# Half as many broadcast rows before a graph attention, over four PSUM banks, with two transfers issued earlier

## The chip, the cores and the metric

The kernel runs on one core of a Trainium2 chip. The metric is the device time of one execution in microseconds (us). TensorE (PE) multiplies matrices, PEld is its weight load, VectorE (DVE), ScalarE (ACT) and GpSimd (POOL) do elementwise work, SyncE (SP) issues the transfers (DMA).

## What is computed

A layer norm over a first graph layer (nodes `x`, 3327 x 128, padded here to 26 tiles of 128 rows, 3328), then a second layer norm over a gated graph attention layer. Only the second layer is touched by the change. Cut to its core:

```python
hp = (adj > 0) @ hW ; hm = (adj < 0) @ hW                      # adj without its diagonal
e_plus  = leaky_relu(concat([hp, hm], 1) @ a, 0.2)[:, 0]       # one number per node and head
e_minus = leaky_relu(concat([hm, hp], 1) @ a, 0.2)[:, 0]
att = where(adj > 0, e_plus[None, :], NEG_INF)
att = where(adj < 0, e_minus[None, :], att)
att = softmax(att, axis=1)
support = sum over 3 heads of (att * adj) @ hW / 3
```

Every entry of `adj` in the given inputs is zero or between 0.05 and 1: none is negative. The kernel computes the right thing for negative entries too, in branches on a flag that is read from the data.

## The kernel before, in words

`program` (L2481) calls three stages one after the other, each a block at whose end all engines meet at a barrier: `layer0` (about 1515 us of the span), `normalize_and_sum` (L1628) and `attention_and_gates` (L2134).

`normalize_and_sum` goes over the 26 row tiles of `adjT`. For each, PE makes the node support (`g_sp`, L1755) and the sums for the scores (`g_ep`, L1777 and L1778), and ACT copies both out in `copy_sums` (L1815 to L1821), into 128 columns of `nsT` and a slice of `raw`, and raises `sums_copied`. That semaphore starts at 2, so it stands at 26 after 24 tiles and at 28 after all. SP loads the tiles (L1714, four buffers), then stores `hT` (L1719), waits for `sums_copied` to reach T + 2 = 28, stores the whole of `nsT` (L1721) and waits until both stores have landed (`stored`), before it goes to the barrier. DVE ends with `epm` (L1918): six numbers per node, three heads for positive entries and three for negative ones.

`attention_and_gates` begins with a spread: `EB` (128 x 6 x 3328) holds for each of the six a row of 3328 numbers, the same on all 128 partitions. PE makes it by transposing a column of `epm` that is broadcast to 128 x 128 against the identity (L2264), up to four transposes into one PSUM bank; such a bank is a group, 7 groups to a row (six of 4 transposes, one of 2), 42 groups. Two banks are used in turn. ACT copies the even groups to `EB` (L2338), DVE the odd ones (L2402). On DVE the copies stand behind the reading of the flag (L2393 to L2397: four register loads and an ALU chain), on PE the first transposes of attention stand behind them and behind the load of `W`. SP issues at the start of this block the first row tile of `adj` (L2217), `W`, the second tile and seven pieces of `adjT`.

Then for each of 26 row tiles and 3 heads: DVE masks the tile (once per tile, `masks`, L2407 to L2422) and makes logits and their maximum (L2436), ACT the exponential (L2347), PE transposes the 128 x 3328 result in seven pieces (L2281), DVE multiplies each with its piece of `adjT` (L2458), and PE multiplies it with `H` (L2322). DVE makes the logits two heads ahead. The first logits wait for the last copy of `EB` and for the first tile of `adj`. In `masks` and `logits` an `If` on the flag holds what negative entries need; with the given inputs it is jumped over. After 26 tiles come the gates (`gates_and_output`), which use `EB` as room.

Of the kernel before, what the change touches and what calls it, by code (L numbers as in the profile page):

```python
# [10 lines left out]
ACT = mybir.ActivationFunctionType  # L11
AX = mybir.AxisListType

P = 128
# [1610 lines left out]
                        taken_batch()  # L1625


def normalize_and_sum(nc, d, dims, H, ident, diag, epm, negs):  # L1628


    N, NP, T = dims
# [4 lines left out]
    with ExitStack() as ctx:  # L1636
# [64 lines left out]
        with nc.Block() as block:  # L1701
            @block.sync
            def _(eng):
                eng.dma_start(X[:, :, :], d["x_rows"]).then_inc(x_loaded, 16)
                eng.dma_start(shift[:, :], d["ln_b"].partition_broadcast(P)).then_inc(x_loaded, 16)
                eng.dma_start(gain[:, :], d["ln_g"].partition_broadcast(P)).then_inc(x_loaded, 16)
                eng.dma_start(WT[:, :, :], d["gat_WT"]).then_inc(loaded, 16)
                eng.dma_start(av[:, :, :], d["gat_a"]).then_inc(loaded, 16)

                def load(r, q):  # L1710
                    t = r * BUFS + q

                    eng.wait_ge(adj_free, t + 1)
                    eng.dma_start(adj[q][:, :], d["adjT"][bass.ds(t * P, P), :]).then_inc(adj_loaded[q], 16)  # L1714

                over_tiles(eng, load)

                eng.wait_ge(hT_ready, NC)
                eng.dma_start(d["hT"], hT[:, :]).then_inc(stored, 16)  # L1719
                eng.wait_ge(sums_copied, T + 2)  # L1720
                eng.dma_start(d["nsT"], nsT[:, :]).then_inc(stored, 16)  # L1721
                eng.wait_ge(stored, 32)

            @block.gpsimd
            def _(eng):
# [405 lines left out]
    return early_loads, late_load_and_stores, products, gates, blends  # L2131


def attention_and_gates(nc, d, dims, H, ident, diag, epm, negs):  # L2134

    N, NP, T = dims
    HEADS = 3
# [7 lines left out]
    with ExitStack() as ctx:  # L2145
        sb, ps, sem = scope(nc, ctx)
        EB = sb("EB", [P, 2 * HEADS, NP])
        adj = [sb(f"a_adj{i}", [P, NP]) for i in range(2)]
        adjT = sb("a_adjT", [P, NP])
        negmask = sb("negmask", [P, NP], mybir.dt.uint8)  # L2150
        prob = [sb(f"prob{i}", [P, NP]) for i in range(HEADS)]
# [16 lines left out]
        acc, rt, sup = acc_bank[:, 0:P], small_bank[:, 0:P], small_bank[:, P:2 * P]  # L2168

        loaded = sem("a_loaded")  # L2170
        adj_loaded = [sem(f"a_adj_loaded{i}") for i in range(2)]
        adjT_loaded = [sem(f"a_adjT_loaded{c}") for c in range(NC)]
        eb_turned = sem("a_eb_turned")
        eb_copied = [sem(f"a_eb_copied{i}") for i in range(2)]
# [13 lines left out]

        early_loads, late_load_and_stores, products, gates, blends = gates_and_output(
            ctx, nc, d, dims, H, ident, diag, EB, [t[:, :] for t in prob], tr + [acc_bank, small_bank], gs_stored, sup_copied)  # L2190
        EB_GROUPS = 2 * HEADS * NC

        def width(c):
            return min(512, NP - c * 512)
# [17 lines left out]
        with nc.Block() as block:  # L2212
            @block.sync
            def _(eng):
                for k in range(2):
                    eng.sem_inc(gs_stored[k], 16)
                eng.dma_start(adj[0][:, :], d["adj"][0:P, :]).then_inc(adj_loaded[0], 16)  # L2217
                eng.dma_start(W[:, :, :], d["gat_W"]).then_inc(loaded, 16)
                eng.dma_start(adj[1][:, :], d["adj"][P:2 * P, :]).then_inc(adj_loaded[1], 16)
                for c in range(NC):  # L2220
                    sl = slice(c * 512, c * 512 + width(c))
                    eng.dma_start(adjT[:, sl], d["adjT"][0:P, sl]).then_inc(adjT_loaded[c], 16)

                def store(p, k):
                    t = p * 2 + k
                    eng.wait_ge(sup_copied, t + 1)
                    eng.dma_start(d["gsT"][:, bass.ds(t * P, P)], gs[k][:, :]).then_inc(gs_stored[k], 16)

                def after(p, k, more_rows, more_turned):
                    if more_rows:  # L2230
                        eng.wait_ge(logit_ready, seq(p, k * HEADS + HEADS - 1) + 1)
                        eng.dma_start(adj[k][:, :], d["adj"][bass.ds((p * 2 + k + 2) * P, P), :])\
                           .then_inc(adj_loaded[k], 16)
                    if more_turned:
                        for c in range(NC):
                            sl = slice(c * 512, c * 512 + width(c))
                            eng.wait_ge(pT_ready, chunk(p, (k * HEADS + HEADS - 1) * NC + c) + 1)
                            eng.dma_start(adjT[:, sl], d["adjT"][bass.ds((p * 2 + k + 1) * P, P), sl])\
                               .then_inc(adjT_loaded[c], 16)

                after(0, 0, True, True)
                store(0, 0)
                after(0, 1, True, True)
                with eng.Fori(1, PAIRS - 1) as p:
                    store(p - 1, 1)
                    after(p, 0, True, True)
                    store(p, 0)
                    after(p, 1, True, True)
                store(PAIRS - 2, 1)
                after(PAIRS - 1, 0, False, True)  # L2250
                eng.wait_ge(logit_ready, seq(PAIRS, 0))
                early_loads(eng)
                store(PAIRS - 1, 0)
                store(PAIRS - 1, 1)
                late_load_and_stores(eng)

            @block.tensor
            def _(eng):
                for g in range(EB_GROUPS):
                    h, c = g // NC, g % NC  # L2260
                    if g >= 2:
                        eng.wait_ge(eb_copied[g % 2], g // 2)
                    for j in blocks(c):
                        mm = eng.transpose(tr[g % 2][:, (j % 4) * P:(j % 4 + 1) * P],  # L2264
                                           epm[:, j, h:h + 1].to_broadcast([P, P]), ident[:, :])
                    mm.then_inc(eb_turned, 1)
                for i in range(2):
                    eng.wait_ge(eb_copied[i], EB_GROUPS // 2)
                eng.wait_ge(loaded, 16)

                def turn(p, g, first, last_read):
# [62 lines left out]
            def _(eng):  # L2334
                for g in range(0, EB_GROUPS, 2):
                    h, c = g // NC, g % NC
                    eng.wait_ge(eb_turned, g + 1)
                    eng.activation(EB[:, h, c * 512:c * 512 + width(c)], tr[g % 2][:, 0:width(c)], ACT.Copy)\  # L2338
                       .then_inc(eb_copied[0], 1)

                def exp(p, n):
# [48 lines left out]
            def _(eng):  # L2390
# [8 lines left out]
                for g in range(1, EB_GROUPS, 2):  # L2399
                    h, c = g // NC, g % NC  # L2400
                    eng.wait_ge(eb_turned, g + 1)
                    eng.tensor_copy(EB[:, h, c * 512:c * 512 + width(c)], tr[g % 2][:, 0:width(c)])\  # L2402
                       .then_inc(eb_copied[1], 1)
                eng.drain()
                eng.wait_ge(eb_copied[0], EB_GROUPS // 2)

                def masks(p, k):  # L2407

# [2 lines left out]
                    block_ = adj[k][:, bass.ds((p * 2 + k) * P, P)]  # L2411
                    with eng.If(eng.snap(flag) > 0):

                        eng.tensor_tensor(dblock[:, :], block_, ident[:, :], ALU.mult)
                        eng.drain()
                        eng.tensor_tensor(block_, block_, dblock[:, :], ALU.subtract)
# [63 lines left out]
def program(nc, d, dims):  # L2480
    N, NP, T = dims  # L2481
    with ExitStack() as ctx:
# [4 lines left out]
        diag = sb("diag", [P, T])  # L2487
        epm = sb("epm", [P, T, 6])
        negs = sb("negs", [P, T])
        normalize_and_sum(nc, d, dims, H, ident, diag, epm, negs)  # L2490
        attention_and_gates(nc, d, dims, H, ident, diag, epm, negs)


# [43 lines left out]
```

## Time and profile before

| | us |
|---|---|
| median of 3 runs | 2671.07 (2668.92 to 2672.51) |
| the profiled execution | 2673.42 |
| its span in the trace | 2671.6 |
| end of `normalize_and_sum`: last copy of sums to the first instruction of attention | 1787.73 to 1793.86 |
| the spread of `epm` into `EB` | 1793.86 to 1824.75 |
| first logits to first transposes of attention | 1825.24 to 1835.16 |
| the attention proper, to the gates | to about 2569 |

Times inside the span are us from its start. Busy shares over the whole span are PE 87%, DVE 80%, ACT 40%; they are averages over stages with different limits, and the change touches two short stretches, so it is read from those stretches. The trace's "issue" is time in which an engine waited for nothing that the profile shows; a q behind an engine's name is its sequencer.

### The profile page before, as it was taken

Reading aid. Unit: us, or ns where it says so; the run is one execution under the profiler, and the core shown is the slowest. Engines: PE = TensorE matmul, PEld = TensorE weight load, DVE = VectorE, ACT = ScalarE, POOL = GpSimd, SP = SyncE. Lnnn points to the kernel's source line nnn. Section 1 sums busy time; section 2 is a strip of 40 time slices with the busy share of each in tenths; the row PEclk is TensorE's granted clock in tenths of the full one; section 3 lists DMA queues with packets and bytes.
Section 4 is the critical chain, followed back from the end, with each engine's and each line's share of the span. In section 5 each row is a group of like instructions: output and inputs, shape, how many; then the busy total and the mean of one; then the engine's idle time right before and its main releaser. Section 6 shows DMA issues by size and latency. Waiting matters only on the chain. (4 is left out here: it accounts for less than half of the span.)

```text
span 2671.6 us, 53662 instructions
## 1 busy us (share of the span) xinstructions
PE 2328.7 (87%) x17795; PEld 1971.7 (74%) x17795; DVE 2145.3 (80%) x6600; ACT 1069.8 (40%) x1803; POOL 156.8 (6%) x342
## 2 busy tenths in 40 slices
PE   7999999879889979988967369987999999999995
PEld 2666666657777867777757369976999999999962
DVE  4777777578787888888889677757999999999956
ACT  5666666443434444334431220004443333444333
POOL 0000000111111111110000100000000000000000
PEclk8999999989999989999988769999999999999997
DMA  4000000022223322222302226542343333433320
GB/s 134 2 2 1 1 1 1 2 103 78 92 91 118 116 78 104 101 80 89 119 27 103 98 96 221 205 175 84 110 142 114 130 130 104 135 125 116 119 92 26
DMA packets 57309, 244.87 MB, mean 92 GB/s; under 512 B 6929, under 2 KB 18576, under 8 KB 43344
## 3 DMA queue, kind: packets, MB, share of 16 engines
q1 hardware_dynamic: 57040, 241.99, 25.9%
q8 instruction: 83, 1.36, 0.2%
q14 instruction: 186, 1.52, 0.2%
HBM read 235.15 MB, written 6.82 MB: 91 GB/s over the span
## 5 line engine op out<-in xcount | busy, mean ns | idle before, releaser
L2322 PE MATMUL a_acc<-H,pT 128*128 128x128 f32 x4056 | 547.8, 277 | 11.6 <-ACT a_rows L2355 3.8
L2322 PEld LDWEIGHTS a_acc<-H,pT 128*128 128x128 f32 x4056 | 495.3, 192 | 28.6 <-DVE pT L2458 20.1
L994 PE MATMUL small<-XR,wT 128*128 128x128 f32 x2756 | 378.5, 283 | 27.3 <-ACT wT L1264 26.7
L994 PEld LDWEIGHTS small<-XR,wT 128*128 128x128 f32 x2756 | 344.3, 197 | 43.2 <-ACT wT L1264 43.2
L865 PE MATMUL lg<-kT,qs 128*128 128x512 f32 (+1 forms) x742 | 339.1, 593 | 27.0 <-ACT e L1182 16.8
L75 DVE MAX8 cand<-e 128x8 f32<-128x64 f32 (+3 forms) x1898 | 303.0, 241 | 50.9 <-issue 27.5
L2458 DVE TENSOR_TENSOR pT<-a_tr,a_adjT 128x512 f32<-128x512 f32 (+1 forms) x546 | 316.6, 645 | 22.2 <-PE a_tr L2281 19.1
L2281 PE MATMUL a_tr<-ident,prob 128*128 128x128 f32 x2028 | 311.4, 274 | 10.9 <-ACTq L2349 10.9
L1264 ACT ACTIVATE wT<-tr 128x512 f32<-128x512 f32 (+1 forms) x371 | 206.5, 566 | 267.3 <-PE tr L984 266.4
L894 PE MATMUL accR<-XR,adj 128*128 128x129 f32 x2704 | 313.4, 276 | 0.0
L894 PEld LDWEIGHTS accR<-XR,adj 128*128 128x128 f32 x2704 | 309.2, 193 | 0.0
L2436 DVE CUSTOM_DVE_ANT_0 prob<-a_adj,EB 128x3328 f32<-128x3328 f32 x78 | 282.6, 3623 | 0.0
L984 PE MATMUL tr<-ident,e 128*128 128x128 f32 x1378 | 216.6, 285 | 59.3 <-DVE scalars L1519 53.5
L865 PEld LDWEIGHTS lg<-kT,qs 128*128 128x128 f32 x742 | 118.4, 193 | 185.7 <-ACT e L1182 142.5
L984 PEld LDWEIGHTS tr<-ident,e 128*128 128x128 f32 x1378 | 168.3, 147 | 110.7 <-DVE scalars L1519 56.2
L1182 ACT ACTIVATE e<-lg 128x512 f32<-128x512 f32 (+1 forms) x371 | 206.6, 566 | 106.7 <-PE lg L865 104.9
L2281 PEld LDWEIGHTS a_tr<-ident,prob 128*128 128x128 f32 x2028 | 241.1, 142 | 11.1 <-issue 11.1
L2347 ACT ACTIVATE prob<-prob,a_negmax 128x3328 f32<-128x3328 f32 x78 | 239.0, 3064 | 9.1 <-DVE a_negmax L2445 9.1
L1755 PE MATMUL g_sp<-g_adj,H 128*128 128x128 f32 x1352 | 162.7, 282 | 17.1 <-ACTq L1820 17.1
L1755 PEld LDWEIGHTS g_sp<-g_adj,H 128*128 128x128 f32 x1352 | 158.5, 198 | 18.8 <-issue 18.2
L1214 ACT ACTIVATE e<-e,scalars 128x3327 f32<-128x3327 f32 x53 | 162.0, 3059 | 8.7 <-DVE scalars L1583 8.6
L224 DVE SCALAR_TENSOR_TENSOR work<-cand,mid 128x416 f32<-128x416 f32 (+1 forms) x172 | 127.3, 774 | 9.8 <-issue 3.2
(351 smaller groups left out, 2427.9 us busy)
## 6 DMA issues: line engine op xcount, KB each, us to landing
adj<-in_adjT SPq DMA_DIRECT2D x52, 1664.0 KB, 7.2
g_adj<-in_adjT SPq DMA_DIRECT2D x26, 1664.0 KB, 7.0
a_adj<-in_adj SPq DMA_DIRECT2D x26, 1664.0 KB, 6.8
a_adjT<-in_adjT SPq DMA_DIRECT2D x156, 256.0 KB, 3.9
a_adjT<-in_adjT SPq DMA_DIRECT2D x26, 128.0 KB, 4.4
XT<-in_x_t SPq DMA_DIRECT2D x1, 1664.0 KB, 7.2
hT_scratch<-hT SPq DMA_DIRECT2D x1, 1664.0 KB, 12.1
nsT_scratch<-nsT SPq DMA_DIRECT2D x1, 1664.0 KB, 5.3
```

What stands on the lines that cost most here:

```text
L75: eng.max(cand[:, n, :], src[:, n * seg:min((n + 1) * seg, width)])
L865: eng.matmul(lg[bank(st, p, k, c)][:, 0:sl.stop - sl.start], qs[k][:, :], kT[:, sl], start=True, stop=True).then_inc(lg_ready, 1)
L894: mm = eng.matmul(accR[:, :], adj[k][:, j * P:(j + 1) * P], xf[:, j, :], start=False, stop=(j == T - 1))
L984: mm = eng.transpose(tr[(k * NC + c) % 2][:, o:o + P], e[b][k][:, j * P:(j + 1) * P], ident[:, :])
L994: mm = eng.matmul(accA[:, :], wT[(k * NC + c - 1) % 2][:, o:o + P], xa[:, j, 0:P], start=(j == 0), stop=(j == T - 1))
L1182: eng.activation(e[b][k][:, sl], lg[bank(st, p, k, c)][:, 0:sl.stop - sl.start], ACT.Copy).then_inc(lg_free, 1)
L1755: mm = eng.matmul(sp[k][:, :], H[:, j, :], adj[q][:, j * P:(j + 1) * P], start=(j == 0), stop=(j == T - 1))
L2281: mm = eng.transpose(tr[g % BANKS][:, (j % 4) * P:(j % 4 + 1) * P], prob[order[n][1]][:, j * P:(j + 1) * P], ident[:, :])
L2322: mm = eng.matmul(acc[:, :], pT[g % RING][:, (j % 4) * P:(j % 4 + 1) * P], H[:, j, :], start=(j == 0), stop=(j == T - 1))
L2347: eng.activation(prob[h][:, :], prob[h][:, :], ACT.Exp, bias=negmax[h][:, :], accum_out=den[h][:, :])
L2436: eng.tensor_tensor_reduce(prob[h][:, :], adj[k][:, :], EB[:, h, :], 1.0, -3.0e38, ALU.add, ALU.max, mx[h][:, :])
L2458: eng.tensor_tensor(pT[g % RING][:, 0:width(c)], tr[g % BANKS][:, 0:width(c)], adjT[:, c * 512:c * 512 + width(c)], ALU.mult).then_inc(pT_ ...
```

## The change

1. `EB_GROUPS` is 3 x 7 = 21 in place of 42: only the three rows for positive entries are spread, over four PSUM banks (`EB_BANKS`) in place of two. ACT copies 11 groups, DVE 10; a group waits for the copy of the group four before it.
2. The rows for negative entries are made by a new function, `spread_minus`, on DVE alone, inside the flagged branch of the first tile's `masks`: three loops, jumped over where the flag is zero.
3. The first row tile of `adj` gets its own buffer, `first_adj`, and its load is issued in the stage before, behind the last load of `adjT` and ahead of the store of `hT`.
4. The store of `nsT` is split: columns 0 to 3071 once `sums_copied` is at 26, the last 256 columns (128 KB) at 28. The wait on `stored` is for all three.

```diff
@@ normalize_and_sum, SP
                 over_tiles(eng, load)
 
+                eng.dma_start(first_adj[:, :], d["adj"][0:P, :]).then_inc(first_adj_loaded, 16)
                 eng.wait_ge(hT_ready, NC)
                 eng.dma_start(d["hT"], hT[:, :]).then_inc(stored, 16)
+                most = NP - 2 * P
+                eng.wait_ge(sums_copied, T)
+                eng.dma_start(d["nsT"][:, 0:most], nsT[:, 0:most]).then_inc(stored, 16)
                 eng.wait_ge(sums_copied, T + 2)
-                eng.dma_start(d["nsT"], nsT[:, :]).then_inc(stored, 16)
-                eng.wait_ge(stored, 32)
+                eng.dma_start(d["nsT"][:, most:NP], nsT[:, most:NP]).then_inc(stored, 16)
+                eng.wait_ge(stored, 48)
@@ attention_and_gates
-        adj = [sb(f"a_adj{i}", [P, NP]) for i in range(2)]
+        adj = [first_adj, sb("a_adj1", [P, NP])]
...
-        EB_GROUPS = 2 * HEADS * NC
+        EB_GROUPS = HEADS * NC
+        EB_BANKS = 4
+        by_engine = [-(-EB_GROUPS // 2), EB_GROUPS // 2]
@@ SP
-                eng.dma_start(adj[0][:, :], d["adj"][0:P, :]).then_inc(adj_loaded[0], 16)
                 eng.dma_start(W[:, :, :], d["gat_W"]).then_inc(loaded, 16)
@@ PE
-                    if g >= 2:
-                        eng.wait_ge(eb_copied[g % 2], g // 2)
+                    if g >= EB_BANKS:
+                        eng.wait_ge(eb_copied[g % 2], (g - EB_BANKS) // 2 + 1)
                     for j in blocks(c):
-                        mm = eng.transpose(tr[g % 2][:, (j % 4) * P:(j % 4 + 1) * P],
+                        mm = eng.transpose(tr[g % EB_BANKS][:, (j % 4) * P:(j % 4 + 1) * P],
                                            epm[:, j, h:h + 1].to_broadcast([P, P]), ident[:, :])
@@ DVE
+                def spread_minus():
+
+                    quarters = [slice(q, q + 32) for q in range(0, P, 32)]
+                    for h in range(HEADS):
+                        with eng.Fori(0, T) as t:
+                            eng.tensor_copy(dblock[:, 0:32], epm[:, bass.ds(t, 1), HEADS + h].to_broadcast([P, 32]))
+                            eng.drain()
+                            eng.transpose(dblock[:, 32:64], dblock[:, 0:32])
+                            eng.drain()
+                            for n, own in enumerate(quarters):
+                                for to in quarters:
+                                    eng.tensor_copy(EB[to, HEADS + h, bass.ds(t * P + 32 * n, 32)], dblock[own, 32:64])
+                            eng.drain()
...
                     with eng.If(eng.snap(flag) > 0):
 
+                        if isinstance(p, int) and p == 0 and k == 0:
+                            spread_minus()
```

On SP, around the end of `normalize_and_sum` and the start of attention, before:

```order
L1714 DMA g_adj<-in_adjT 128x3328 [waits g_adj_free] x2
L1719 DMA hT_scratch<-hT 128x3328 [waits g_hT_ready]
L1721 DMA nsT_scratch<-nsT 128x3328 [waits g_sums_copied]
L1701 UNCONDITIONAL_BRANCH [waits g_stored]
L2213 UNCONDITIONAL_BRANCH [waits barrier_Pool_Activation_PE_DVE_SP_release]
L2217 DMA a_adj<-in_adj 128x3328
L2218 DMA gat_W_s<-in_gat_W 128x384
L2219 DMA a_adj<-in_adj 128x3328
```

and now:

```order
L1714 DMA g_adj<-in_adjT 128x3328 [waits g_adj_free] x2
L1718 DMA first_adj<-in_adj 128x3328
L1720 DMA hT_scratch<-hT 128x3328 [waits g_hT_ready]
L1723 DMA nsT_scratch<-nsT 128x3072 [waits g_sums_copied]
L1725 DMA nsT_scratch<-nsT 128x256 [waits g_sums_copied]
L1701 UNCONDITIONAL_BRANCH [waits g_stored]
L2219 UNCONDITIONAL_BRANCH [waits barrier_Pool_Activation_PE_DVE_SP_release]
L2223 DMA gat_W_s<-in_gat_W 128x384
L2224 DMA a_adj<-in_adj 128x3328
```

The first tile's load has moved ahead of the barrier and of the store of `hT`, and most of the store of `nsT` stands on a wait of its own. On DVE, at the start of attention, before:

```order
L66 TENSOR_LOAD a_flag_int x4
L67 ISA
L2402 COPY EB<-a_tr 128x512 [waits a_eb_turned] x6
L2402 COPY EB<-a_tr 128x256 [waits a_eb_turned]
L2402 COPY EB<-a_tr 128x512 [waits a_eb_turned] x6
L2402 COPY EB<-a_tr 128x256 [waits a_eb_turned]
L2402 COPY EB<-a_tr 128x512 [waits a_eb_turned] x6
L2402 COPY EB<-a_tr 128x256 [waits a_eb_turned]
L2410 MEMSET a_gate 128x1 [waits a_adj_loaded0,a_eb_copied0]
L2412 COMPARE_AND_BRANCH
```

and now (the list goes on with the three loops of `spread_minus`; with them the branch jumps over about 117 instructions in place of 3):

```order
L66 TENSOR_LOAD a_flag_int x4
L67 ISA
L2407 COPY EB<-a_tr 128x512 [waits a_eb_turned] x6
L2407 COPY EB<-a_tr 128x256 [waits a_eb_turned]
L2407 COPY EB<-a_tr 128x512 [waits a_eb_turned] x3
L2429 MEMSET a_gate 128x1 [waits first_adj_loaded,a_eb_copied0]
L2431 COMPARE_AND_BRANCH
L2416 UNCONDITIONAL_BRANCH
L2416 ISA
L2417 COPY a_dblock<-epm 128x32
L2419 STREAM_TRANSPOSE a_dblock<-a_dblock 128x32
```

Eleven of DVE's 21 copies are gone, and the branch behind them is longer. On PE the first groups, before and now:

```order
L2264 MATMUL a_tr<-ident,epm 128x128 x8
L2264 MATMUL a_tr<-ident,epm 128x128 [waits a_eb_copied0]
L2264 MATMUL a_tr<-ident,epm 128x128 x3
L2264 MATMUL a_tr<-ident,epm 128x128 [waits a_eb_copied1]
L2264 MATMUL a_tr<-ident,epm 128x128 x3
```

```order
L2269 MATMUL a_tr<-ident,epm 128x128 x16
L2269 MATMUL a_tr<-ident,epm 128x128 [waits a_eb_copied0]
L2269 MATMUL a_tr<-ident,epm 128x128 x3
L2269 MATMUL a_tr<-ident,epm 128x128 [waits a_eb_copied1]
L2269 MATMUL a_tr<-ident,epm 128x128 x3
```

Sixteen transposes, four groups, now stand ahead of the first wait for a copy, where it was eight.

## Rows read from the trace of the kernel before

**Rows 1.** The page: the span, and the busy time of each engine.

```profile
span 2671.6 us, 53662 instructions
PE 2328.7 (87%) x17795; PEld 1971.7 (74%) x17795; DVE 2145.3 (80%) x6600; ACT 1069.8 (40%) x1803; POOL 156.8 (6%) x342
```

**Rows 2.** Stretches: us, busy PE, PEld, DVE, ACT, POOL, PEclk, DMA share, GB/s.

```profile
1793.80:1797.00 3.20, 2.89 (x12) 2.28 (x12) 0.99 (x6) 0.82 (x2) 0.00 (x0) 0.50 0.54 147
1797.00:1800.00 3.00, 1.96 (x14) 1.47 (x14) 1.51 (x3) 1.06 (x3) 0.00 (x0) 0.94 0.98 406
1805.00:1810.00 5.00, 4.25 (x28) 2.65 (x27) 2.50 (x4) 2.21 (x5) 0.00 (x0) 1.00 0.83 314
1900.00:2000.00 100.00, 98.73 (x871) 96.53 (x869) 92.88 (x139) 38.79 (x48) 0.00 (x0) 1.00 0.36 123
```

**Rows 3.** SP's own waits, 1760 to 1850: total, times, longest.

```profile
SPq L1701 <- DMA nsT_scratch<-nsT: 5.0, 1, 5.0
```

**Rows 4.** Timeline of the boundary: start, us, work [idle before <- releaser].

```profile
1788.13 0.32 SPq L1721 DMA_DIRECT2D nsT_scratch<-nsT  x1
1788.14 0.32 DVE L1913 TENSOR_TENSOR esum<-raw_e 128x156 f32<-128x156 f32 x1 [10.66 <-ACTq L1820]
1788.95 0.32 DVE L1918 SCALAR_TENSOR_TENSOR epm<-esum 128x156 f32<-128x156 f32 x1
1793.86 2.89 PE L2264 MATMUL a_tr<-ident,epm 128*128 128x128 f32 x12 [6.18 <-PEq L1701]
1794.98 0.60 ACT L2338 ACTIVATE EB<-a_tr 128x512 f32<-128x512 f32 x1 [6.90 <-PE a_tr L2264]
1796.83 0.69 DVE L2402 COPY EB<-a_tr 128x512 f32<-128x512 f32 x1 [1.81 <-PE a_tr L2264]
```

**Rows 5.** Chain of waits, one round of the spread: start, us, what.

```profile
1797.58 0.66 PE a_tr L2264 x4
1798.26 0.70 DVE EB L2402
```

**Rows 6.** Timeline: PE at full clock, and two ACT copies back to back.

```profile
1797.58 1.09 PE L2264 MATMUL a_tr<-ident,epm 128*128 128x128 f32 x8 [0.83 <-DVE EB L2402]
1555.02 1.08 ACT L1813 ACTIVATE hT<-g_tp 128x512 f32<-128x512 f32 x2
```

**Rows 7.** Timeline of DVE, end of the spread and the first logits; PE behind them.

```profile
1824.95 0.06 DVE L2410 MEMSET a_gate<- 128x1 f32 x1 [0.20 <-issue]
1825.24 1.89 DVE L2420 TENSOR_SCALAR a_adj<-a_adj 128x3328 f32<-128x3328 f32 x1 [0.23 <-issue]
1835.16 4.35 PE L2281 MATMUL a_tr<-ident,prob 128*128 128x128 f32 x24 [10.86 <-ACTq L2349]
```

**Rows 8.** Landing times: L1996 (128 x 256, from scratch), L2217 (128 x 3328), L1719 (the store of hT).

```profile
L1996 SPq DMA_DIRECT2D EB<-gsT_scratch x1: 339/339/339, 2571.1 to 2571.1; - x1
DMA to landing us min/median/max: 2.1/2.1/2.1
DMA to landing us min/median/max: 6.8/6.8/6.8
DMA to landing us min/median/max: 12.1/12.1/12.1
```

**Rows 9.** Timeline of DVE behind branches that jump over long pieces of code.

```profile
52.77 0.16 DVE L168 TENSOR_SCALAR scalars<-scalars 128x2 f32<-128x2 f32 x1 [7.94 <-issue]
600.46 3.69 DVE L464 SCALAR_TENSOR_TENSOR e<-work,scalars,e 128x3328 f32<-128x3328 f32 x1 [0.73 <-issue]
675.86 3.69 DVE L464 SCALAR_TENSOR_TENSOR e<-work,scalars,e 128x3328 f32<-128x3328 f32 x1 [2.22 <-issue]
```

**Rows 10.** normalize_and_sum, 1700 to 1790: the loads of g_adj; DVE's last tile.

```profile
L1714 SPq DMA_DIRECT2D g_adj<-in_adjT x7: 332/333/339, 1704.3 to 1755.9; - x7
1769.63 0.29 DVE L1845 TENSOR_TENSOR dblock<-g_adj,ident 128x128 f32<-128x128 f32 x1
```

More of the change, by code:

```diff
@@ L1625, in _, with normalize_and_sum @@
                         taken_batch()
-def normalize_and_sum(nc, d, dims, H, ident, diag, epm, negs):
+def normalize_and_sum(nc, d, dims, H, ident, diag, epm, negs, first_adj, first_adj_loaded):
     N, NP, T = dims
@@ L2131, in gates_and_output, with attention_and_gates @@
     return early_loads, late_load_and_stores, products, gates, blends
-def attention_and_gates(nc, d, dims, H, ident, diag, epm, negs):
+def attention_and_gates(nc, d, dims, H, ident, diag, epm, negs, first_adj, first_adj_loaded):
     N, NP, T = dims
@@ L2170, in attention_and_gates @@
         loaded = sem("a_loaded")
-        adj_loaded = [sem(f"a_adj_loaded{i}") for i in range(2)]
+        adj_loaded = [first_adj_loaded, sem("a_adj_loaded1")]
         adjT_loaded = [sem(f"a_adjT_loaded{c}") for c in range(NC)]
@@ L2267, in _ @@
                 for i in range(2):
-                    eng.wait_ge(eb_copied[i], EB_GROUPS // 2)
+                    eng.wait_ge(eb_copied[i], by_engine[i])
                 eng.wait_ge(loaded, 16)
@@ L2337, in _ @@
                     eng.wait_ge(eb_turned, g + 1)
-                    eng.activation(EB[:, h, c * 512:c * 512 + width(c)], tr[g % 2][:, 0:width(c)], ACT.Copy)\
+                    eng.activation(EB[:, h, c * 512:c * 512 + width(c)], tr[g % EB_BANKS][:, 0:width(c)], ACT.Copy)\
                        .then_inc(eb_copied[0], 1)
@@ L2401, in _ @@
                     eng.wait_ge(eb_turned, g + 1)
-                    eng.tensor_copy(EB[:, h, c * 512:c * 512 + width(c)], tr[g % 2][:, 0:width(c)])\
+                    eng.tensor_copy(EB[:, h, c * 512:c * 512 + width(c)], tr[g % EB_BANKS][:, 0:width(c)])\
                        .then_inc(eb_copied[1], 1)
                 eng.drain()
-                eng.wait_ge(eb_copied[0], EB_GROUPS // 2)
+                eng.wait_ge(eb_copied[0], by_engine[0])
+                def spread_minus():
[10 more added lines that the diff above has]
+                            eng.drain()
                 def masks(p, k):
@@ L2489, in program @@
         negs = sb("negs", [P, T])
-        normalize_and_sum(nc, d, dims, H, ident, diag, epm, negs)
-        attention_and_gates(nc, d, dims, H, ident, diag, epm, negs)
+        first_adj, first_adj_loaded = sb("first_adj", [P, NP]), sem("first_adj_loaded")
+        normalize_and_sum(nc, d, dims, H, ident, diag, epm, negs, first_adj, first_adj_loaded)
+        attention_and_gates(nc, d, dims, H, ident, diag, epm, negs, first_adj, first_adj_loaded)
 def kernel(x, adj, L0_gnn_W1, L0_gnn_W2, L0_gnn_W3, L0_gnn_U1, L0_gnn_U2, L0_gnn_ln_g, L0_gnn_ln_b,
```

## The prediction

> **What bounds the kernel now.** I read the page first: over the whole span PE is busy 87%, DVE 80%, ACT 40% [rows 1]. That says only that most of the time is matmul. So I went to the stretches next. In attention proper PE is busy 98.73 of 100 us at the full granted clock [rows 2]; nothing in the change touches what PE does there. The spread of `epm` into `EB` ahead of it is another matter: in 1805 to 1810 PE is busy 4.25 of 5 us, DVE 2.50, ACT 2.21, so no engine is full. Who holds it is seen in the chain of waits: four transposes (0.66 us until DVE can start), a DVE copy (0.70), the next four transposes, which wait for that copy because its bank is theirs [rows 5]. A round trip of 1.36 us plus about 0.07 for the semaphores makes 1.43 us per two groups. Two banks are the bound, not PE and not the copies. The timeline gives the whole: PE starts at 1793.86 [rows 4], and DVE, behind its last copy, goes on at 1824.95 [rows 7]. That is 31.1 us from PE's start. After it comes a serial stretch that the change leaves alone: masks, two logits and an exponential until PE's first transposes of attention at 1835.16, PE idle for 10.86 us [rows 7]. Since nothing later waits for anything but this chain, what the spread gets shorter, the end gets earlier.
>
> Ahead of the spread lies the barrier. `epm` is done at 1789.27, yet PE starts only at 1793.86 [rows 4]: SP waited 5.0 us for the store of `nsT`, issued at 1788.13 [rows 3, 4].
>
> **The spread, 21 groups over four banks.** All times from PE's first transpose. PE now has 3 x 26 = 78 transposes. At the full clock a transpose costs 0.11 us: eight in 1.09 us, of which about 0.27 is the last one's way through the array, leave 0.82 for seven steps [rows 6]. At the start the granted clock is 0.50, its lower level of 1.2 GHz, after 6.18 us in which PE did nothing, and in 1797 to 1800, with PE busy since 1793.86, it is 0.94 as a mean, so it rose near 1797.4, 3.5 us after the start [rows 2, 4]. The first group of four took from 1793.86 to ACT's start at 1794.98, 1.12 us, less 0.33 for the last one's way: 0.24 each [rows 4]. So 3.5 / 0.24 = 15 transposes are done at the lower clock and the other 63 take 63 x 0.11 = 6.9: PE ends at 10.4 if it never waits.
>
> Does it wait? A group comes back to a bank after three others, 3 x 0.44 = 1.3 us at the full clock, and a copy with its semaphores and the way through the array needs about 0.70 + 0.07 + 0.24 = 1.0 [rows 5]. It fits. DVE is late at the start: it reads the flag first and its first copy begins 2.97 us after PE's start [rows 4]. That copy is of group 1, and the first group that needs its bank is group 5, at about 3.5 + 0.5 = 4.0; the copy ends at 3.66. It fits too, by 0.3 us. The copies themselves: DVE has 10 of 0.69 at most, 6.9 us after 2.97; ACT has 11, two of them in 1.08 us back to back [rows 6]. PE is the bound, then. Behind its end come the way through the array and one short copy on ACT, 0.24 + 0.38, and the handover to DVE: 11.1 in all. **The spread falls from 31.1 to 11.1 us: 20.0 us off.** Of this the 78 transposes that go away are worth 14 groups and more, and the banks the rest; I don't need to part them.
>
> Bounds: if the rate were not PE's 0.11 but, with some waits left, the 0.14 of eight in 1.09 read as it stands, 63 x 0.03 = 1.9 us less is won. If PE kept the full clock through a shorter idle time, DVE's late first copy would hold group 5 at 3.7 and only 0.2 more is won. So 18 to 20.2.
>
> **The barrier.** The store that is left for the end is 128 x 256. The nearest row is a load of that very shape from scratch memory, 2.1 us from issue to landing [rows 8]; the whole store took 5.3, that is up to 1793.4, 0.4 before the release [rows 3, 4]. Issued at 1788.13 it lands at 1790.2, behind DVE's end at 1789.27. **3.2 us off.** Bounds: 0 if the small store took as long as the large one; 4.1 if DVE's end alone decided. The large part waits for 24 tiles, about 16 us before the end (two tiles are left, and seven loads stand 8.6 us apart [rows 10]). It must be through by 1788, and is even behind a long queue: the last `adjT` tile, `first_adj` and `hT` are three transfers of 1664 KB issued from 1755.9. At 5.3 us each they are through by 1772 and the part of `nsT` by 1778: ten us to spare.
>
> **What the early load pushes.** `first_adj` now stands beside the last `adjT` tile and ahead of `hT`. `hT` was already slow, 12.1 us [rows 8], and its reader comes 770 us later. The last `adjT` tile is wanted by DVE at 1769.63 [rows 10], 13.7 us after its issue at 1755.9; three transfers at 5.3 us each, wholly shared, would be through 15.9 us after it, at worst 2.2 us late. DVE then has 10.66 us without work behind that tile [rows 4], so I cost this at nothing. The gain of the early load itself: in its old place it would have landed 6.8 us after its issue [rows 8], about 7.3 after PE's start, against 11.1 when DVE first wants it. It is hidden anyway: nothing. `W`, the second tile and `adjT` move up by one transfer in the queue and are wanted behind PE's first transposes of attention, 10 us and more after the spread's end [rows 7]: nothing.
>
> **The longer branch.** The first `If` jumps over some 117 instructions in place of 3. Before, MEMSET to the masks took 0.29 us, 0.23 of it idle [rows 7]. In `layer0`, DVE's gap between a match and the selection behind it, where three branches jump over pieces of up to 80 instructions, is 0.73 us in one case and 2.22 in another [rows 9]. I take the lower, **0.5 us more than before**, and keep 0 and 2.0 as ends. The Trainium skill (Runtime: NRT & Kernel Launch, Instruction fetch mechanics) says that a taken branch whose target lies outside the two pages of code held forces a fetch. By that rule the cost here is all or nothing; whether this jump leaves the pages I can't see from before, and the 0.73 and 2.22 for like code agree with such a rule.
>
> **Sum.** -20.0 - 3.2 + 0.5 = -22.7 us. Against the profiled execution, 2673.42 - 22.7 = 2650.7; its span would be 2648.9. The median of the runs is 2.35 below that execution, so I forecast 2671.07 - 22.7 = **2648.4 us**, ratio 0.9915. The bounds of the three terms together (-18 to -20.2, 0 to -4.1, 0 to 2.0) would give 2646.8 to 2655.1.
>
> **Rivals.**
> 1. *The barrier gives nothing* (the small store lands as late, or another engine is late there). For it: a landing time has a fixed part that I know from a load only. Price 3.2: 2651.6. Chance 8%.
> 2. *The jump is a fetch.* For it: 2.22 and the 7.94 us at another change of code [rows 9]. Price 2 to 4 instead of 0.5: 2650 to 2652. Chance 15%.
> 3. *PE stays at its lower clock through the spread.* It works in pieces there. All 78 at 0.24 give 18.7 + 0.7: 19.4 in place of 11.1, so 2656.7. Against it: with PE at work only 70% of the time, the clock was at 1.00 from 1800 on [rows 2, 6]. Chance 3%.
> 4. *DVE's loop in attention moves in code memory* and its jump back (11 rounds of two tiles) turns into a fetch. DVE is busy 92.88 of 100 us [rows 2], so with a round of 56 us it has 4.0 us to spare; only a stall above that holds PE up. At 7.94 us, the longest code gap [rows 9], 11 x 3.9 = 43 us are lost against 22.7 won: 2691, slower than before. It decides the sign from 4.0 + 22.7 / 11 = 6.1 us a round. Against it: the loop is about 230 instructions, and no such gap is seen in attention now. Chance 2%.
> 5. *The gain is given back*: attention starts earlier, into transfers that have not landed. `adjT` is first wanted over 10 us after the spread's end, 21 us after its issue: price 0, unless the queue is slow. With rival 4, 1% of no change.
>
> My forecast holds 72%. The range should reach over rivals 1 and 2 and a few runs' spread (2668.92 to 2672.51, 1.8 each way): 2644.8 to 2654. A difference of 0.2%, 5.3 us, is what a measurement of this kernel can tell from no change. All but rival 4 and the last case are faster by more: faster 0.97, same 0.01, slower 0.02.
>
> **What would show it.** In the changed kernel's trace: 21 copies to `EB`, PE's 78 transposes almost without a gap, the first masks about 11 us after PE's first transpose; SP's wait at the barrier about 2 us in place of 5.0; the gap ahead of the first masks 0.7 in place of 0.23; PE's idle time before attention still about 11 us, and 98.7 busy in 100 after. It is wrong if gaps of over a us stand in the spread, if the end comes earlier by less than the first logits do, or if DVE shows gaps by issue in attention's loop.

## The result, and the profile after

The changed kernel takes 2644.02 us (median of 4, 2642.56 to 2651.45) where the kernel before takes 2669.99 beside it (median of 4, 2664.8 to 2672.51): a ratio of 0.9903, 95% interval 0.989 to 0.9916. It is faster, as forecast, by 26 us and not by 22.7, and 2644.02 lies 0.8 us under the range. Measured twice more, each time beside the kernel before, the same kernel gave 2648.83 (5 runs) and 2644.77 (4), against 2671.72 and 2668.74: 22.9 and 24.0 less.

The page of the changed kernel's profile, its span and the engines, which answers to [rows 1]; the profiled execution took 2642.56 us:

```profile
span 2640.7 us, 53486 instructions
PE 2305.4 (87%) x17717; PEld 1954.3 (74%) x17717; DVE 2136.2 (81%) x6589; ACT 1064.1 (40%) x1793; POOL 152.4 (6%) x342
```

PE has 78 matmul records fewer, DVE 11 instructions. The two spans differ by 30.9 us, more than I said and more than the medians differ. The first question is where those lie. This is the timeline of the changed kernel around the end of `normalize_and_sum` (start, us, work, idle before and releaser), against [rows 4, 7]:

```profile
1780.17 0.28 ACT L1822 ACTIVATE nsT<-g_sp 128x128 f32<-128x128 f32 x1 [7.53 <-PEq L1783]
...
1780.57 0.32 SPq L1725 DMA_DIRECT2D nsT_scratch<-nsT  x1
...
1785.76 2.78 DVE L2407 COPY EB<-a_tr 128x512 f32<-128x512 f32 x4 [1.81 <-PE a_tr L2269]
...
1793.76 0.06 DVE L2429 MEMSET a_gate<- 128x1 f32 x1 [0.20 <-issue]
1794.41 1.90 DVE L2441 TENSOR_SCALAR first_adj<-first_adj 128x3328 f32<-128x3328 f32 x1 [0.59 <-issue]
```

The last copy of sums, after which the changed stretch begins, came at 1780.17; in the first profile of before it came at 1787.73. So 7.6 us of the 30.9 lie ahead of everything the change touches but the place of a load and the first part of a store (issued at 1748.77 and 1764.67). From there on it goes as forecast. SP's own waits at the barrier, against [rows 3]:

```profile
SPq L1701 <- DMA nsT_scratch<-nsT: 1.4, 1, 1.4
```

and the chain of waits through the spread, against [rows 5], in which one row stands for what were alternating pieces:

```profile
1782.75 0.04 issue
1782.79 10.05 PE a_tr L2269 x76
1792.85 0.02 issue
1792.87 0.69 DVE EB L2407
```

PE is the bound now, for 76 of its 78 transposes. One short wait for a bank is left in this profile, too short to leave a gap in PE's own records. It is a weight load that stood 0.23 us for DVE's late first copy; the two later profiles of the same kernel do not have it:

```profile
1786.50 6.31 PEld L2269 LDWEIGHTS a_tr<-ident,epm 128*128 128x128 f32 x58 [0.23 <-DVE EB L2407]
```

I put every profile of the study on the same marks. The columns are: the start of the last copy of sums; from it to PE's first transpose of the spread; from that to the first masks; from the last copy of sums to PE's first transposes of attention, which is the whole changed stretch; and from those to the last copy of `a_gs`.

| profile | last copy | to spread | spread to masks | whole stretch | attention |
|---|---|---|---|---|---|
| before, first | 1787.73 | 6.13 | 31.38 | 47.43 | 734.0 |
| before, again (e6) | 1783.93 | 6.12 | 31.36 | 47.39 | 734.0 |
| after, first | 1780.17 | 2.62 | 11.62 | 24.16 | 734.0 |
| after, again (e7) | 1783.15 | 2.54 | 11.61 | 24.06 | 734.0 |
| after, third (e12) | 1782.86 | 2.53 | 11.62 | 24.06 | 733.9 |
| e1 split store alone | 1785.45 | 2.90 | 31.36 | 44.18 | 734.0 |
| e2 two banks | 1786.64 | 2.61 | 17.93 | 30.46 | 734.0 |
| e3 all six rows | 1786.08 | 2.54 | 19.83 | 32.29 | 734.0 |
| e4 short branch | 1782.87 | 2.54 | 11.25 | 23.70 | 734.0 |
| e5 late load | 1789.00 | 2.90 | 11.63 | 24.45 | 734.0 |
| e8 head 0 first | 1791.76 | 2.64 | 6.94 | 20.22 | 733.5 |
| e10 the same again | 1778.50 | 2.61 | 5.94 | 18.84 | 733.9 |
| e9 PE kept busy | 1789.63 | 2.62 | 11.72 | 24.26 | 733.9 |
| e11 both | 1784.85 | 3.00 | 5.94 | 19.23 | 733.9 |

The last column shows that nothing behind the stretch moved by over 0.5 us in any kernel, and behind the last `a_gs` all have 102.4 to 102.5 us left. What differs is the stretch, and the first column.

### The profile page after: what moved, and what is told of

It is laid out like the page before. It is cut to its first block and busy times, and to the rows that moved or that the text cites. A ratio compares the mean times of both kernels' runs of the same rounds, so it can differ in the third digit from the quotient of the medians.

```text
span 2640.7 us, 53486 instructions
## 1 busy us (share of the span) xinstructions
PE 2305.4 (87%) x17717; PEld 1954.3 (74%) x17717; DVE 2136.2 (81%) x6589; ACT 1064.1 (40%) x1793; POOL 152.4 (6%) x342
## 5 line engine op out<-in xcount | busy, mean ns | idle before, releaser
L2286 PEld LDWEIGHTS a_tr<-ident,prob 128*128 128x128 f32 x2028 | 242.0, 142 | 11.5 <-issue 11.5
L2457 DVE CUSTOM_DVE_ANT_0 prob<-first_adj,EB 128x3328 f32<-128x3328 f32 x39 | 141.3, 3622 | 0.0
L2457 DVE CUSTOM_DVE_ANT_0 prob<-a_adj,EB 128x3328 f32<-128x3328 f32 x39 | 141.2, 3621 | 0.0
```

The lines of the kernel that those rows point to most:

```text
L2286: mm = eng.transpose(tr[g % BANKS][:, (j % 4) * P:(j % 4 + 1) * P], prob[order[n][1]][:, j * P:(j + 1) * P], ident[:, :])
L2457: eng.tensor_tensor_reduce(prob[h][:, :], adj[k][:, :], EB[:, h, :], 1.0, -3.0e38, ALU.add, ALU.max, mx[h][:, :])
```

## The experiments

**The same two kernels again (e6, e7, e12).** No edit. The question was whether the 7.6 us ahead of the stretch belong to the change.

> The kernel before, once more, for its stretches and its clock. In the first pair of profiles the last copy of sums ended normalize_and_sum at 1787.73 (before) and 1780.17 (after), though no instruction ahead of it differs except loads on SP: 7.6 us that my sum did not have. Theory A (chance of the granted clock): this run's copy falls anywhere between 1778 and 1790, two executions of one kernel differ by several us there, and the gaps between tile copies are either 8.35 or 9.97 us. Theory B (the change makes that stage faster, by where buffers or code lie): the copy comes at 1787 to 1789 here, with the same two gaps of 9.97. Time within 1.8 us of the kernel before by either.

> The changed kernel once more. From the last copy of sums to the first transposes of attention both theories expect 23.4 us less than before (24.0 where 47.4 was, within 0.5). Theory A: the last copy of sums anywhere in 1778 to 1790, the time in five rounds 22 to 25 us under the kernel before. Theory B: the copy at 1780 to 1781, the time 28 to 31 us under the kernel before.

> The changed kernel a third time, beside the three others of this call. Theory A (the rest of the first pair's difference was the clock's chance): from the last copy of sums to PE's first transposes of attention 24.1 us within 0.3, the copy itself anywhere from 1778 to 1790, the time 22 to 24 us under the kernel before.

The kernel before, run again, took 2669.54 us (11 runs) and its last copy came at 1783.93: 3.8 us earlier than in its own first profile. The changed kernel's came 3.0 us later than in its first. The gaps between copies of sums, in the timeline of ACT, in the first profile of before:

```profile
1737.94 0.28 ACT L1818 ACTIVATE nsT<-g_sp 128x128 f32 x1 [7.62 <-PEq L1779]
1747.91 0.28 ACT L1818 ACTIVATE nsT<-g_sp 128x128 f32 x1 [9.61 <-PEq L1779]
```

and the same two copies in the second:

```profile
1735.77 0.28 ACT L1818 ACTIVATE nsT<-g_sp 128x128 f32 x1 [7.62 <-PEq L1779]
1744.11 0.28 ACT L1818 ACTIVATE nsT<-g_sp 128x128 f32 x1 [7.99 <-PEq L1779]
```

A tile takes 9.97 us in one and 8.34 in the other, in one and the same kernel. (Most tiles take 7.9 to 8.0 us in every profile; the 8.34 or 9.97 come at every fourth.) The granted clock differs with it: in the first it fell during that tile (stretches, columns as in [rows 2]),

```profile
1736.00:1742.00 6.00, 5.00 (x74) 4.92 (x73) 4.62 (x6) 0.35 (x2) 0.00 (x0) 0.78 0.48 158
1742.00:1745.00 3.00, 3.00 (x26) 3.00 (x25) 2.49 (x6) 0.00 (x0) 0.00 (x0) 0.88 0.60 257
```

and in the second it didn't:

```profile
1738.00:1748.00 10.00, 9.37 (x124) 9.29 (x123) 8.02 (x8) 0.35 (x2) 0.00 (x0) 1.00 0.65 240
```

Before, first, had two such long tiles, before, again, none; the three profiles of the changed kernel had none, but its relatives e3, e5 and e2 had two, two and one. The two long tiles are 3.3 of the 7.6 us. The rest lies ahead of the first copy of sums, which came at 1583.76 in the first profile of before and at 1579.45 in the first of the change. Most of it is the projection, 52 multiplications of PE, 128x9 each. In the kernel before (its row of the timeline, then a stretch inside it, columns as in [rows 2]):

```profile
1562.91 11.27 PE L1762 MATMUL g_yp<-V,hT 128*128 128x9 f32 x52 [0.54 <-ACT hT L1813]
1563.00:1574.00 11.00, 11.00 (x52) 11.00 (x53) 1.43 (x2) 0.00 (x0) 0.00 (x0) 0.50 0.01 1
```

and in the change:

```profile
1561.34 9.13 PE L1766 MATMUL g_yp<-V,hT 128*128 128x9 f32 x52 [0.72 <-ACT hT L1817]
1561.00:1570.00 9.00, 8.66 (x51) 8.67 (x51) 1.85 (x2) 0.28 (x2) 0.00 (x0) 0.65 0.01 2
```

That is 2.1 us at a granted clock of 0.50 against 0.65, and 0.6 more in the first tile behind it. The kernel before, run again, took 9.01 us for the same 52. The last 1.6 us were there before the projection, 1.3 of them by the end of `layer0`, which lies 2.5 us apart in the two profiles of before; I did not follow them. So theory A holds as far as it goes: the time ahead of the stretch varies by several us in either kernel, some 6.0 of the 7.6 us here with the clock, and the first pair happened to be far apart. The three profiles of the changed kernel all lie earlier than the two of before (1780.2 to 1783.2 against 1783.9 and 1787.7), but e5, which has nearly the same code, had 1789.0; an effect of 1 or 2 us of the change on this part is not excluded. Of the other expectations that of e6's time was missed: 2.2 us under the same kernel beside it (2671.72), not within 1.8, with an interval of 0.998 to 0.9998 for the ratio of one kernel to itself. So 2 us between medians mean nothing here. The others held: the stretch is 23.3 us shorter (47.4 to 24.1, 24.2 in the first profile), and the medians of e7 and e12 are 22.9 and 24.0 us under the kernel before.

**The barrier (e1).** Kernel before, with this alone:

```diff
+                most = NP - 2 * P
+                eng.wait_ge(sums_copied, T)
+                eng.dma_start(d["nsT"][:, 0:most], nsT[:, 0:most]).then_inc(stored, 16)
                 eng.wait_ge(sums_copied, T + 2)
-                eng.dma_start(d["nsT"], nsT[:, :]).then_inc(stored, 16)
-                eng.wait_ge(stored, 32)
+                eng.dma_start(d["nsT"][:, most:NP], nsT[:, most:NP]).then_inc(stored, 16)
+                eng.wait_ge(stored, 48)
```

> The kernel before with the store of nsT split, and nothing else. My forecast had 3.2 us for it, from a landing time of 2.1 us; in the changed kernel PE's first transpose came 2.6 us after the last copy of sums where 6.1 had been, 3.5 less. Theory (the barrier waited for the large store alone): 3.5 us less between these two, the rest unchanged. Rival (the early load, or another part, gave it): less than 1 us.

2667.13 us (10 runs) beside 2670.3 (15 runs): 3.2 less, ratio 0.9988, interval 0.9976 to 1.0, so the runs alone hardly tell it from the 2.2 us that e6 had without an edit. In the trace the way to the spread is 2.90 us in place of 6.12, the stretch 44.18 in place of 47.4. SP's wait:

```profile
SPq L1701 <- DMA nsT_scratch<-nsT: 1.3, 1, 1.3
```

The small store's wait is 1.3 us where the whole one's was 5.0 [rows 3]. It gives 3.2 us alone, a little less than the 3.5 expected; the rival fell. The last 0.3 to 0.4 us, 2.90 down to 2.54, appear in those kernels that also load the first tile early (e5, without it, has 2.90 again); I did not find through what.

**Groups and banks (e2, e3).** The changed kernel with `EB_BANKS = 2`; and with `EB_GROUPS = 2 * HEADS * NC`, four banks and no `spread_minus`.

> The changed kernel with two banks for the spread in place of four. Theory (round trip of a bank): two groups take 1.43 us as before, so the spread of 21 groups takes 3 us for DVE's late start plus some 18 groups at 0.72, about 16 us from PE's first transpose to DVE's first masks in place of 11; 4.9 us slower than the change. Rival (PE is the bound in either, and what counted was the number of transposes): 11 us, no slower.

> The changed kernel with all six rows spread by PE (42 groups) over four banks, and without the loops in the flagged branch. Theory (with four banks PE is the bound at 0.11 us a transpose): 78 transposes more, 8.5 us longer than the change, some 19.5 us from PE's first transpose to the masks, and 0.4 us back for the shorter branch. Rival (the banks still hold it): 1.43 us per two groups, 31 us, 20 us slower.

e2 took 2658.47 us, 13.3 under the kernel before beside it (ratio 0.996, interval 0.9945 to 0.9975), e3 2655.87, 15.9 under it (0.9941, 0.9926 to 0.9956). The chain of waits of e2 shows the old round trip:

```profile
1796.01 0.70 DVE EB L2407
...
1796.76 0.74 PE a_tr L2269 x4
...
1797.52 0.70 DVE EB L2407
...
1798.27 0.66 PE a_tr L2269 x4
```

and PE's timeline in e3 one unbroken piece:

```profile
1788.62 18.88 PE L2269 MATMUL a_tr<-ident,epm 128*128 128x128 f32 x156 [2.60 <-PEq L1701]
```

156 transposes in 18.88 us and no wait, twice the work of the change for 8.2 us more to the masks, or 8.6 without the shorter branch, near the 8.5 forecast. With two banks the spread costs 17.93 us, 6.3 more than with four and 1.4 more than I expected, as the first round trips fall into a time at the lower clock (0.50 in 1792 to 1795). Both theories held in kind, both rivals fell. From 31.4 us, half the groups alone takes off 13.4, four banks alone 11.5, both together 19.8: after either one the other is worth less.

**The branch (e4).** The call of `spread_minus` is left out, so the rows for negative entries would be missing if there were any.

> The changed kernel without spread_minus in the flagged branch, so that rows for negative entries are not made (no entry is negative here). Theory (the long jump costs the gap seen ahead of the first masks): the gap of 0.59 us there falls to 0.23, 0.4 us in all, too little for the median to tell. Rival (code length shifts something else, above all in DVE's loop): the attention part differs by over 1 us.

2645.88 us, ratio 0.9913 (0.9893 to 0.9933), not to be told from the three medians of the change. In the traces the way from spread to masks is 11.25 in place of 11.61: 0.36 us, which is the gap by issue of 0.59 ahead of the masks in the change less the 0.23 of [rows 7]. Attention is 734.0 in either: no stall came with the new place of DVE's loop in the code, in either.

**The early load (e5).** `first_adj` is loaded at the start of attention again.

> The changed kernel with the first row tile loaded where it was, at the start of attention. Theory (hidden anyway): it lands 6.8 us after an issue 0.45 us behind PE's first transpose, against 10.9 us when DVE wants it, so nothing: the masks start at the same distance, within 0.2 us. Rival (with a spread this short it is late, as the queue begins with three transfers): the masks wait 1 to 3 us.

The masks start 11.63 us after PE's first transpose, 11.61 with the early load. It is hidden anyway, as forecast. The time, 2651.9 us (2648.76 to 2653.52, ratio 0.9932, 0.9911 to 0.9953), is nevertheless 3 to 8 us above the changed kernel's three medians, and all four runs of e5 (2648.76 and up) took longer than all four of e4 (up to 2647.96), measured beside them. Its profile puts this ahead of the stretch: the last copy at 1789.00, with the projection at 11.27 us and two long tiles. I take it for the clock's chance, but four runs do not show that. A rival stays open: that the early load, which shifts the transfers of that stage, has an effect on how often its tiles are long. Of the profiles without it (before twice, e1, e5) three had two long tiles and one none; of the ten with it, five had none.

**DVE waits for head 0 only (e8, e10).** The changed kernel with DVE copying groups 1, 3 and 5 alone and starting behind head 0's groups. `copied_up_to(g)` is how many of the groups up to g are ACT's:

```diff
+        own_groups = {1: [1, 3, 5]}
+        own_groups[0] = [g for g in range(EB_GROUPS) if g not in own_groups[1]]
...
-                eng.wait_ge(eb_copied[0], by_engine[0])
+                eng.wait_ge(eb_copied[0], copied_up_to(NC - 1))
...
+                    if isinstance(p, int) and p == 0 and 0 < n < HEADS:
+                        eng.wait_ge(eb_copied[0], copied_up_to((n + 1) * NC - 1))
```

> The changed kernel with DVE copying only groups 1, 3 and 5 and waiting only for head 0's seven groups before its first logits; ACT copies the other 18, and the logits of heads 1 and 2 wait for theirs. Theory (DVE's chain from the spread to the exponential is what sets the start of attention, PE and ACT have room beside it): masks start some 5.7 us after PE's first transpose in place of 11, and ACT is through with its copies and its table load near 12.5, just as the first exponential is wanted: 4.5 to 5.4 us faster than the change. Rival (ACT becomes the bound): the exponential starts late by up to 2 us, and 3 us are won.

> The kernel in which DVE waits only for head 0's rows, once more: in its first profile the clock rose 5.8 us after PE's first transpose where the change had 3, and the masks began at 6.9. Theory (chance of the clock, again): masks between 5.6 and 7.0 us after PE's first transpose, and the first transposes of attention 3.8 to 5.0 us earlier against the last copy of sums than in the change, so 19 to 20.3 us; the time 4 us under the change's in this call.

The stretch is 20.22 and 18.84 us where the change has 24.1: 3.9 and 5.3 us off. The masks start at 6.9 and 5.9. In e8 the clock still stood at its lower level up to 1800, 5.6 us after PE's start at 1794.40, where in e10 it had risen 3 us after it; that goes with the 1.2 us over the 5.7 of my sum (stretches of e8):

```profile
1798.00:1800.00 2.00, 2.00 (x12) 2.00 (x11) 0.96 (x3) 0.60 (x1) 0.00 (x0) 0.50 1.01 426
```

The rival is half right: ACT is a little late. In e10 it goes from its copies through the table load into the exponential without a pause, and begins that at 1794.01, the maximum of the logits having been ready at 1793.60:

```profile
1784.99 7.71 ACT L2352 ACTIVATE EB<-a_tr 128x512 f32<-128x512 f32 x16 [0.45 <-PE a_tr L2278]
1792.71 1.28 ACT L2361 ACT_TABLE_LOAD   x1
1794.01 3.07 ACT L2361 ACTIVATE prob<-prob,a_negmax 128x3328 f32<-128x3328 f32 x1
```

The medians are 2644.33 (5 runs) and 2644.17 (4 runs, 2635.47 to 2647.07); the change beside the second had 2644.77 (the first had no run of the change beside it). So the traces show 4 to 5 us in the stretch, and the runs, with their spread ahead of it, do not show that the whole kernel is faster. The expectations were missed by a little in the stretch (e8 4.5 to 5.4 us off, e10 19 to 20.3 us long), and that of 4 us under the change's time altogether.

**PE kept busy (e9, e11).** 84 transposes of the identity while PE waits for the first normalized rows, 16 before the second half; e11 also has 20 behind the last tile, on top of e10. Their results are not used. The first of them:

```diff
+                eng.wait_ge(mean_ready, 3)
+                for n in range(84):
+                    eng.transpose(sp[0][:, :], ident[:, :], ident[:, :])
...
```

> The changed kernel with PE kept busy in normalize_and_sum while it waits for the normalized rows: 84 transposes of the identity into a free bank ahead of the first transposes of H, 16 more ahead of the second half; their results are not used. Theory (what differs between profiles of one kernel ahead of the change is how long PE runs at its lower clock, and the projection there runs at it for most of its length): the granted clock from the first transposes of H on is 1.00 where it is 0.50 to 0.84, the 52 records of the projection take 6 us in place of 9 to 11, the first copy of sums comes at 1574 to 1577 in place of 1579 to 1586, and the kernel is 4 to 8 us faster than the change. Rival (the projection waits for DVE or for its weights, not for the clock): under 1 us.

> That kernel with PE kept busy in both places: the 100 transposes of the identity of e9_warm, and 20 more behind the last tile of normalize_and_sum, while the engines meet at the barrier. Theory: the clock stays at 1.00 through the spread, the masks begin 5.2 us after PE's first transpose, ACT is through with its copies and its table load by then plus 6, so the first transposes of attention come 18.3 to 19 us after the last copy of sums; with the gain of e9_warm 9 to 13 us faster than the change. Rival (20 transposes delay the barrier, or the clock falls in the barrier all the same): no less than e10 plus e9 give.

e9 took 2652.04 us (2647.9 to 2653.12), 7 more than the change beside it; the theory fell. PE in e9:

```profile
1541.21 12.12 PE L1747 MATMUL g_sp<-ident 128*128 128x128 f32 x84 [12.02 <-DVEq L1839]
1554.97 1.09 PE L1756 MATMUL g_tp<-ident,H 128*128 128x128 f32 x8 [1.64 <-DVEq L1899]
...
1563.99 8.25 PE L1772 MATMUL g_yp<-V,hT 128*128 128x9 f32 x52 [0.69 <-ACT hT L1823]
1572.10 8.66 PE L1765 MATMUL g_sp<-g_adj,H 128*128 128x128 f32 x52
```

The first transposes of `H` did run at the full clock, 1.09 us for eight where the change took 1.97. But they wait for DVE anyway, and the clock then fell during the projection itself (stretches of e9):

```profile
1565.00:1570.00 5.00, 5.00 (x36) 5.00 (x35) 0.90 (x2) 0.00 (x0) 0.00 (x0) 0.73 0.02 3
1570.00:1575.00 5.00, 5.00 (x24) 5.00 (x25) 2.26 (x7) 0.00 (x0) 0.00 (x0) 0.50 0.00 0
```

The first copy of sums came at 1582.12, as in the change (1579.45 to 1582.43), and four tiles of the loop then were long ones, 6.6 us in all. Whether the busy work brought those about or chance, one profile does not tell. e11 took 2643.66, the change beside it 2644.77, where 9 to 13 us were expected; its stretch, 19.23, is no shorter than e10's, and the 20 transposes cost the barrier 0.4 us. The clock did stay at 1.00 from those 20 transposes into the spread, and bought nothing: PE was through its first 20 transposes in 2.37 us and then stood until DVE's late first copy gave a bank free,

```profile
1791.56 6.62 PE L2286 MATMUL a_tr<-ident,epm 128*128 128x128 f32 x58 [1.35 <-DVE EB L2424]
```

3.7 us after its start, as the prediction's bounds had it.

## Why the prediction was right, and where it was wrong

**What bounds the kernel** was right: the spread was held by two banks in turn (e2, e3), the barrier by one store (e1), and what came off there came off at the end, as attention and the gates kept their 734.0 and 102.4 to 102.5 us.

**The spread.** 20.0 us were forecast. From PE's first transpose to DVE's MEMSET it is 1793.76 - 1782.79 = 11.0 where I had 11.1: 20.1 came off. The bound is as forecast, but the closeness of the total is in part luck, for several steps of it were a little off. A transpose at the lower clock was put at 0.24 us. The 0.79 us left of the first group give 0.26 over three steps or 0.20 over four, and in the changed kernel ACT's first two copies, eight transposes apart, start 1.70 us apart, 0.21 each:

```profile
1783.92 0.60 ACT L2343 ACTIVATE EB<-a_tr 128x512 f32<-128x512 f32 x1 [3.40 <-PE a_tr L2269]
1785.62 0.60 ACT L2343 ACTIVATE EB<-a_tr 128x512 f32<-128x512 f32 x1 [1.11 <-PE a_tr L2269]
```

The clock rose near 3 us in and not at 3.5. So PE was through at 10.26 us where the sum had 10.64 with the last one's way. The end, however, came from DVE's last long copy (from 1792.87, 0.69 us, and 0.20 to the MEMSET) and not from ACT's short one, and lay 0.7 us behind PE in place of 0.5. The late first DVE copy (2.97 us behind PE's start in either kernel) was to fit by 0.3 us; it held a weight load up for 0.23 in the first profile and nothing in the other two. The 0.11 at the full clock, read from 0.82 over seven, which is 0.117, proved right: e3's 78 further transposes took 8.62 us.

**The barrier.** 3.2 forecast, 3.5 to 3.6 measured in the whole change (6.13 to 2.62, 2.54 and 2.53), 3.2 in e1. The small store landed sooner than the load of its shape, 2.1 us, from which its time was taken:

```profile
nsT_scratch<-nsT SPq DMA_DIRECT2D x1, 128.0 KB, 1.8
```

**The branch.** +0.5 forecast, +0.36 measured. The rival in which the jump costs 2 to 4 us did not come about. The fetch rule that the prediction cites from the Trainium skill (Runtime: NRT & Kernel Launch, Instruction fetch mechanics) is neither confirmed nor refuted by a jump that cost 0.36 us: no run shows whether it left the pages held.

**The early load** was costed at nothing, and is worth nothing within the stretch, where it should have shown (e5), save perhaps for 0.3 us at the barrier. What it does to the tiles ahead of the stretch is open, as said at e5.

The sum, -22.7, stands against -23.3 in the traces (47.4 to 24.1, in three profiles of the change and two of before) and against medians of -26.0, -22.9 and -24.0. No rival came about. Against the third, that PE stays at its lower clock, the prediction said that PE was at work only 70% of the time; the rows it names have 4.25 of 5 us, 85%.

**The step that failed** is the range, and in it the term "a few runs' spread (2668.92 to 2672.51, 1.8 each way)". Three runs of one kernel were no measure of its spread. Over the study the kernel before ran from 2663.54 to 2676.05 and the change from 2642.56 to 2656.12, 12.5 and 13.6 us. Medians are steadier, but the three of the changed kernel still lie 4.8 us apart. The profiles put what varies in stages that the change leaves alone, most of it where the granted clock differs. In the first comparison the kernel before was near its usual 2670 and the changed kernel had the lowest of its three medians: of the 26.0 us, 23.3 are the stretch and 2.7 lie outside it. The sum was also 0.6 too small (0.3 at the barrier, 0.1 each in the spread and the branch). Put together, 2648.4 is missed by 4.4 us: 1.1 because the kernel before had 2669.99 and not 2671.07 beside it, 0.6 from the sum, 2.7 from outside the stretch. With the sum right the lower end would have been 2644.2, still too high; with half of the 12.5 us in place of 1.8 it would have been 2640.5. The stated ends are not quite those of the prediction's own numbers either: 2646.8 less 1.8 is 2645.0, and its upper bound of 2655.1 lies above the 2654 given.

The trace of before held a sign that I passed over: gaps of 8.35 and of 9.97 us for the same work in one loop.

## What to carry to other kernels

Where a producer fills PSUM banks in turn and each is emptied by one copy, compare the round trip (fill, semaphore, copy, semaphore) with the number of banks times the fill: here the round trip is 1.43 us and a fill of four transposes 0.44, so two banks (0.88) were too few and four (1.76) are enough. Two groups took 1.43 us before and take 0.88 now, at no cost in instructions. A barrier behind a large store is shortened by storing what is ready ahead of it, down to the time of the small one that is left, here 1.8 us for 128 KB where the whole took 5.3. And judge a change of some 20 us in 2650 by marks in the trace around it: for the kernel before and for the change they agreed within 0.1 us where whole runs of one kernel lay 12 to 14 us apart. Take more than one profile even so, for e8 and e10 are one kernel and their stretches lie 1.4 us apart.

## What the runs showed of the hardware that I had not expected

- The same loop over the same data has tiles of 8.34 or of 9.97 us, with the granted clock at 1.00 in the one and below it in the other; among 14 profiles of near kernels 0 to 4 tiles of the loop over 26 were long ones, and one kernel had two in one profile and none in another.
- The granted clock fell from 0.95 in 1560 to 1565 to 0.50 in 1570 to 1575 in e9, though PE's records show 5.00 busy us of 5 in between; PE was at multiplications of 128x9 then, and had done 84 transposes in 12.12 us before.
- ACT's copies out of PSUM overlap when they follow each other: 13 of 128x512 and 3 of 128x256 took 7.71 us in e10, where at 0.60 and 0.38 us, as they take alone, they would add up to 8.9.
